# A layernorm's mean and gain applied by VectorE and ScalarE instead of by one matmul a slice

## The reference

```
q, v, g = xn @ Wq, xn @ Wv, xn @ Wg
s[t]  = sigmoid(beta) * s[t-1] + v[t]            # along the sequence, one beta per head
y     = q * s
y     = (y - mean(y)) * rsqrt(var(y) + 1e-5) * ln_g + ln_b     # over the 1024 features
out1  = (y * silu(g)) @ Wo
out2  = mixture of experts of xn: 64 experts, the 8 best per token, two 1024 x 384 up matrices,
        one 384 x 1024 down matrix, silu(h1) * h2; at most 128 token slots per expert
out   = x + out1 + out2
```

## Time and profile before

| what | value |
|---|---|
| median of 3 runs | 2562.5 us |
| the profiled execution | 2563.26 us |
| its span, first to last instruction | 2561.6 us |
| TensorE matmul busy | 2499.2 us, 98% |
| VectorE busy | 1641.4 us, 64% |
| ScalarE busy | 1320.4 us, 52% |
| GpSimd busy | 679.1 us, 27% |
| mean DMA rate | 236 GB/s |
| TensorE's granted clock | 0.991 of full speed |

### The profile page before, as it was taken

How to read it: one execution, slowest core, us unless ns; L and a number is a source line. 1 busy time by engine, 2 the same in 40 slices (tenths; PEclk the granted TensorE clock), 3 DMA queues, 4 the chain that set the end, 5 groups by cost and what they waited for, 6 DMA issues and landing times.

```text
span 2561.6 us, 39307 instructions
## 1 busy us (share of the span) xinstructions
PE 2499.2 (98%) x13625; PEld 2214.0 (86%) x13625; DVE 1641.4 (64%) x1725; ACT 1320.4 (52%) x1499; POOL 679.1 (27%) x523
## 2 busy tenths in 40 slices
PE   7999999899999999999999999999999999999997
PEld 6888977898889988899888898888988889988897
DVE  6776798665566656666665666656665566656654
ACT  4556422464446644556444555545654456544554
POOL 2221122123222222321333222322233232323311
PEclk9999999999999999999999999999999999999998
DMA  7785754696667967669766698666985668866686
GB/s 264 253 296 186 238 202 151 219 312 215 218 219 242 293 235 226 214 221 315 245 230 203 201 317 266 208 212 206 295 286 192 224 220 277 271 227 226 196 269 166
DMA packets 151791, 605.75 MB, mean 236 GB/s; under 512 B 20592, under 2 KB 37040, under 8 KB 151216
## 3 DMA queue, kind: packets, MB, share of 16 engines
q1 hardware_dynamic: 116304, 518.91, 56.5%
q0 software_dynamic: 35424, 86.00, 16.3%
HBM read 520.89 MB, written 100.70 MB: 243 GB/s over the span
## 4 chain that ended last, share of the span: by engine, by line
PE 87%; DVE 7%; ACT 2%; DMA 2%; issue 1%; POOL 0%; SPq 0%; DVEq 0%; ACTq 0%; POOLq 0%
PE psA L1509 17%; PE psA L1511 17%; PE psA L1510 17%; PE psH L1509 7%; PE psH L1511 6%; PE psH L1510 6%; PE psY L1509 4%; PE psY L1511 4%; PE psY L1510 3%; PE psX L1616 2%; PE psY L1541 2%; DVE top L1112 1%; PE psX L1636 1%; DVE keys L1118 1%; DVE pw_lo L1123 1%
## 5 line engine op out<-in xcount | busy, mean ns | idle before, releaser
L1128 DVE TENSOR_TENSOR ew_lo<-ew_raw,ew_hi 128x1536 fp32r<-128x1536 f32 x384 | 693.5, 1816 | 340.8 <-ACT ew_hi L742 326.7
L742 ACT ACTIVATE ew_hi<-ew_raw 128x1536 fp32r<-128x1536 f32 x384 | 568.2, 1483 | 156.4 <-DMA ew_raw<-ew_dram 118.6
L1509 PE MATMUL psA<-xT_hi,pw_hi 128*128 128x512 f32 x1536 | 621.2, 404 | 9.3 <-DVE xT_lo L1043 4.8
L736 ACT ACTIVATE pw_hi<-pw_raw 128x1024 fp32r<-128x1024 f32 x254 | 266.2, 1060 | 672.9 <-PE psA L1511 671.8
L1511 PE MATMUL psA<-xT_hi,pw_lo 128*128 128x512 f32 x1536 | 610.3, 397 | 0.0
L1510 PE MATMUL psA<-xT_lo,pw_hi 128*128 128x512 f32 x1536 | 606.3, 395 | 0.0
L1123 DVE TENSOR_TENSOR pw_lo<-pw_raw,pw_hi 128x1024 fp32r<-128x1024 f32 x256 | 313.4, 1234 | 176.4 <-ACT pw_hi L736 170.4
L1509 PE MATMUL psH<-ew_hi,gT_hi 128*128 128x384 f32 x1024 | 353.3, 345 | 7.9 <-DVE ew_lo L1128 7.1
L1509 PEld LDWEIGHTS psA<-xT_hi,pw_hi 128*128 128x128 f32 x1536 | 290.6, 189 | 72.2 <-DVE xT_lo L1043 5.0
L1511 PEld LDWEIGHTS psA<-xT_hi,pw_lo 128*128 128x128 f32 x1536 | 291.4, 190 | 70.4
L1510 PEld LDWEIGHTS psA<-xT_lo,pw_hi 128*128 128x128 f32 x1536 | 294.0, 191 | 64.0
(11 more groups left out here) (163 smaller groups left out, 3358.4 us busy)
## 6 DMA issues: line engine op xcount, KB each, us to landing
ew_raw<-ew_dram SPq DMA_DIRECT2D x384, 768.0 KB, 6.3
pw_raw<-proj_w_dram SPq DMA_DIRECT2D x256, 512.0 KB, 5.2
xn_scratch<-xt SPq DMA_DIRECT2D x33, 512.0 KB, 4.8
xt<-x_dram SPq DMA_DIRECT2D x32, 512.0 KB, 6.0
out_dram<-x_dram SPq DMA_DIRECT2D x32, 512.0 KB, 6.2
out_dram<-ot POOLq DMA_DIRECT2D x32, 512.0 KB, 12.5
xn<-xn_turned SPq DMA_DIRECT2D x29, 512.0 KB, 4.0
xn_turned<-xraw SPq DMA_DIRECT2D x28, 512.0 KB, 5.1
```

Source lines behind the costliest of these rows:

```text
L736: act.activation(dst[:, slot, :, :], pw_raw[:, slot, :, :], ACT.Copy).then_inc(s_pwhi, 1)
L742: act.activation(ew_hi[:, c % 3, :], ew_raw[:, c % 3, :], ACT.Copy).then_inc(s_ewhi, 1)
L1128: dve.tensor_tensor(ew_lo[:, c % 3, :], ew_raw[:, c % 3, :], ew_hi[:, c % 3, :].bitcast(F32), ALU.subtract).then_inc(s_ewlo, 1)
L1509: pe.matmul(dst, l_hi, r_hi_, start=first, stop=False)
```

## The change

In place of ln6T there is `sel`, two stationary tiles of ones, made once (GpSimd sets four columns, TensorE transposes two tiles, ScalarE copies them). Two matmuls a block (`spread`) multiply them by tok6T, so that bank 0 of psY holds each token's mean on all 128 partitions and bank 1 its deviation. Per slice VectorE then subtracts bank 0 from yb (`center`), ScalarE writes bank 1 times ln_b into `bs`, a buffer of two tiles in SBUF (`std_of`), and `shift_in` computes yb * ln_g + bs. A subtraction is issued one slice ahead of the shift that uses it. The waits on s_sh and s_t move from `shift` on TensorE to `std_of` on ScalarE; the wait of output_mm on the eighth shift stays. The cut diff; the hunks of blocks 0 and 1 place the calls as the text says there: std_of right after gate from slice 3 on in block 0 (0 and 1 after the router step of slice 2), and after gate in block 1.

```diff
+            pool.wait_ge(s_clear, 1)
+            for i in range(2):
+                for r in (0, 2):
+                    o = pool.memset(sel0[:, i, 3 * i + r:3 * i + r + 1], 1.0)
+            o.then_inc(s_clear, 1)
...
+            def std_of(j, m):
+                if isinstance(m, int) and m == 0:
+                    act.wait_ge(s_sh, j + 1)
+                if m >= 2:
+                    act.wait_ge(s_t, KC * j + m - 1)
+                ps = psH if isinstance(j, int) and j == 0 else psY
+                act.activation(bs[:, m % 2, :], ps[:, 1, :], ACT.Copy, scale=ln_b[:, m:m + 1]).then_inc(s_bs, 1)
...
                 gate(j, 2)
+                std_of(j, 0)
+                std_of(j, 1)
                 z_hi_of(j, 0)
                 z_hi_of(j, 1)
                 G(5)
                 gate(j, 3)
+                std_of(j, 2)
+                std_of(j, 3)
                 z_hi_of(j, 2)
                 hidden_part(e + 1)
                 G(6)
                 gate(j, 4)
+                std_of(j, 4)
+                std_of(j, 5)
                 hT_hi_of(e + 1)
                 z_hi_of(j, 3)
                 piece_hi(e + 2, 0)
                 G(7)
                 gate(j, 5)
+                std_of(j, 6)
+                std_of(j, 7)
                 z_hi_of(j, 4)
...
+            def center(j, m):
+                ps = psH if isinstance(j, int) and j == 0 else psY
+                dve.tensor_tensor(yb[:, m, :], yb[:, m, :], ps[:, 0, :], ALU.subtract).then_inc(s_u, 1)
+
             def shift_in(j, m):
-                dve.wait_ge(s_sh, KC * j + m + 1)
-                ps = psH if isinstance(j, int) and j == 0 else psY
-                dve.scalar_tensor_tensor(yb[:, m, :], yb[:, m, :], ln_g[:, m:m + 1], ps[:, m % 2, :],
+                if m == 0:
+                    dve.wait_ge(s_sh, j + 1)
+                    center(j, 0)
+                if m + 1 < KC:
+                    center(j, m + 1)
+                dve.wait_ge(s_u, KC * j + m + 1)
+                dve.wait_ge(s_bs, KC * j + m + 1)
+                dve.scalar_tensor_tensor(yb[:, m, :], yb[:, m, :], ln_g[:, m:m + 1], bs[:, m % 2, :],
                                          ALU.mult, ALU.add).then_inc(s_t, 1)
...
-            def shift(j, m):
-                if m > 1:
-                    pe.wait_ge(s_t, KC * j + m - 1)
+            def spread(j):
+                pe.wait_ge(s_t6, j + 1)
                 ps = psH if isinstance(j, int) and j == 0 else psY
-                pe.matmul(ps[:, m % 2, :], ln6T[:, m, :], tok6T[:, :], start=True, stop=True
-                          ).then_inc(s_sh, 1)
+                for i in range(2):
+                    o = pe.matmul(ps[:, i, :], sel[:, i, :], tok6T[:, :], start=True, stop=True)
+                o.then_inc(s_sh, 1)
...
-                pe.wait_ge(s_t6, j + 1)
                 pe.wait_ge(s_ys, e + 1)
-                shift(j, 0)
-                shift(j, 1)
+                spread(j)
                 g_proj(j, 3)
-                shift(j, 2)
-                shift(j, 3)
                 hidden_mm(e + 1)
                 g_proj(j, 4)
                 hidden_turn(e + 1)
-                shift(j, 4)
-                shift(j, 5)
                 g_proj(j, 5)
-                shift(j, 6)
-                shift(j, 7)
                 g_proj(j, 6)
                 pe.wait_ge(s_t, KC * (j + 1))
```

More of the change, by code:

```diff
@@ L123, in build @@
         tok6T = place("tok6T", [P, TB], F32R)
-        ln6T = place("ln6T", [P, KC, P], F32R)
+        sel = place("sel", [P, 2, P], F32R)
+        bs = place("bs", [P, 2, TB], F32)
         xn = place("xn", [P, KC, P], F32)
@@ L168, in build @@
         top8 = place("top8", [P, 8], F32)
-        ln2 = place("ln2", [P, 2, KC], F32)
-        ln2_hi = place("ln2_hi", [P, 2, KC], F32R)
-        ln6 = place("ln6", [P, KC, P], F32)
+        sel0 = place("sel0", [P, 2, P], F32)
         l1 = place("l1", [P, SLOTS], F32)
@@ L240, in build @@
         s_t6 = sem("s_t6")
-        s_ln = sem("s_ln")
         s_lnT = sem("s_lnT")
@@ L244, in build @@
         s_sh = sem("s_sh")
+        s_u, s_bs = sem("s_u"), sem("s_bs")
         s_t = sem("s_t")
@@ L552, in _ @@
             pool.memset(mk[:, :, :], 0.0)
-            pool.memset(ln6[:, :, :], 0.0).then_inc(s_clear, 1)
+            pool.memset(sel0[:, :, :], 0.0).then_inc(s_clear, 1)
+            pool.wait_ge(s_clear, 1)
[3 more added lines that the diff above has]
+            o.then_inc(s_clear, 1)
             inv_std(3)
@@ L831, in _ @@
                     act.wait_ge(s_lnT, 1)
-                    act.activation(ln6T[:, :, :], chunks(psX), ACT.Copy).then_inc(s_l6, 1)
+                    act.activation(sel[:, :, :].rearrange("p i c -> p (i c)"), psX[:, 0, 0:2 * P], ACT.Copy).then_inc(s_l6, 1)
             square(0, KC // 2 - 1, 1)
@@ L836, in _ @@
                 gate(0, m)
+                if m >= 3:
+                    std_of(0, m - 1)
+                if m == KC - 1:
+                    std_of(0, m)
                 router_step(NTILE - KC + m)
@@ L840, in _ @@
                 if m == 2:
+                    std_of(0, 0)
+                    std_of(0, 1)
                     z_hi_of(0, 0)
@@ L882, in _ @@
                     rows6(1)
+                if m == 2:
+                    std_of(1, 0)
+                if m >= 2:
+                    std_of(1, m - 1)
+                if m == KC - 1:
+                    std_of(1, m)
                 if m == 2:
@@ L1222, in xT_lo_of @@
                                   ALU.subtract).then_inc(s_xlo, 1)
[L1224 to L1237, removed]
             stats_tile(0)
@@ L1282, in _ @@
                 if p == 0:
-                    gain_rows()
                     shift_of(3)
@@ L1684, in _ @@
                 if p == 1:
-                    pe.wait_ge(s_ln, 3)
+                    pe.wait_ge(s_clear, 2)
                     pe.wait_ge(s_plo, NT + 1)
-                    for k in range(KC):
-                        o = pe.transpose(psX[:, k // 4, (k % 4) * P:(k % 4 + 1) * P], ln6[:, k, :], ident[:, :])
+                    for i in range(2):
+                        o = pe.transpose(psX[:, 0, i * P:(i + 1) * P], sel0[:, i, :], ident[:, :])
                     o.then_inc(s_lnT, 1)
@@ L1694, in _ @@
                     token_sums(0)
-                elif m > 2:
-                    shift(0, m - 1)
                 router_step(NTILE - KC + m)
@@ L1700, in _ @@
                 elif m == 2:
[L1701 to L1704, removed]
+                    spread(0)
             for mm in range(KC // 2):
@@ L1726, in _ @@
                 elif m == 2:
[L1727 to L1732, removed]
+                    spread(1)
             pe.wait_ge(s_lf, 1 + SLOTS // 8)
```

## The result

| | before | after |
|---|---|---|
| median of 4 runs | 2563.6 us (2560.4 to 2565.0) | 2609.9 us (2607.7 to 2611.5) |
| ratio, 95% interval | | 1.0187 [1.0174, 1.0199] |
| span of the profiled execution | 2561.6 us | 2605.9 us |
| pitch of the steady blocks (mean of five) | 327.84 us | 334.25 us |

Slower, as forecast, but by 46.3 us where I had said 29.9, and outside my range.

What follows compares the result with a forecast made beforehand. TensorE, busy for 98% of the span, was taken as the bound. Six steady blocks 24.0, block 1 4.9, block 0 and set-up 1 sum to 29.9 us; on 2562.5 that gives 2592 us, range 2574 to 2603.

Steps and rivals of the forecast that it cites:

- First wait: Gate stage of blocks 2 to 7, before the expert's weight piece 3: TensorE would go on 2.7 us later.
- Second wait: Blocks 2 to 7: output product waits until shifts leave psY; 2.3 us wait, both delays together +4.0 us a block.
- Do shifts take turns with GpSimd?: Blocks 2 to 7: scalar_tensor_tensor was to wait for GpSimd, 0.74 up to 1.8 us; sign: some take 1.3 us or more.
- Sum of the two waits: Gate stage of blocks 2 to 7: +4.0 us a block, 24.0 us in six blocks.
- Blocks 0 and 1: Block 1: eight VectorE subtractions on the path to the gather, +4.9 us; block 0 and set-up: std copies and others, +1.
- The pitch of 332: Distance between token transposes of consecutive steady blocks (2 to 7) was to grow from 328 to 332 us.
- Only the second wait grows: Blocks 2 to 7: piece 3 as late as now, output product 1.3 us later a block; 2576 us, chance 0.12.
- matmuls only: Blocks 2 to 7: waits covered, 48 matmul slots saved, 11.0 us faster, 2551.5 us; chance 0.05.
- z_lo(4) wins: Blocks 2 to 7: GpSimd's z_lo(4) gets ahead of gate product 5, a further 1 us a block; 2598 us, chance 0.1.
- The shifts don't take turns: Blocks 2 to 7: shifts are not held by GpSimd, 18.6 us in six blocks; 2587 us, chance 0.2.

Runs made afterwards that it cites:

- experiment 2: Changed kernel with GpSimd's z_lo of slices 0 to 2 held back until VectorE has split piece 3, blocks 2 to 7: 2599.6 us, 1.0144.
- experiment 7: Piece 3 first: expert's piece 3 split ahead of shifts 2 and 3, blocks 2 to 7; changed kernel 2565.5 us (1.0014), kernel before 2553.2 us (0.9969).
- 8: Changed kernel with three moves (weight split before z_hi, shifts 6 and 7 early, piece 3 first): 2556.4 us; silu and hidden product also ahead of piece 5: 2547.8 us.
- Experiment 1: The fill: changed kernel with 14 unused matmuls between the expert's pieces 2 and 3 in blocks 2 to 7: 2594.3 us, 1.0134.
- 4: Changed kernel with ScalarE's weight split, gate 3 and std copies 2 and 3 ahead of z_hi(0) and (1), blocks 2 to 7: 2601.5 us, 1.0164.
- experiment 3: Kernel before plus eight unused VectorE subtractions a block: 1.0189; kernel before plus eight unused ScalarE copies a block: 0.9994.

## Why the prediction was wrong

By its own steps, the predicted 29.9 us against the spans' 44.3:

- **First wait.** Predicted: TensorE goes on 2.7 us later. Measured: 3.05 - 0.47 = 2.58. The chain was the one described: ScalarE's split at 756.70 stands behind z_hi and no longer behind TensorE, GpSimd's z_lo at 756.28 holds VectorE's split for 0.9 us. Removing the turns (experiment 2) gave back 1.1 us.

```profile
755.56 1.24 ACT L804 ACTIVATE z_hi<-yb 128x512 fp32r<-128x512 f32 x2 [3.37 <-DVE yb L1220]
756.70 1.04 ACT L740 ACTIVATE pw_hi<-pw_raw 128x1024 fp32r<-128x1024 f32 x1
```

- **Second wait.** Predicted 2.3 us, net of slots +1.3; measured 2.01 and +1.08. Right, a little too large.
- **Do shifts take turns with GpSimd?** Yes, but they lose less than I gave them. The pair of shifts 6 and 7 takes 1.85 us in block 2 where two undisturbed ones take some 1.4 (0.67 from start to start, 0.75 the last), and the longest of all 64 is 1184 ns, not 1.3 us or more; before, with one operand in PSUM, the maximum was 747:

```profile
L1213 DVE SCALAR_TENSOR_TENSOR yb<-yb,ln_g,bs x64: 739/748/1184, 220.0 to 2459.5; 128x512 f32<-128x512 f32 x64
```

Shift 6 starts at 787.99, while GpSimd has a z_lo from 787.13 to 788.62. The rule of the Trainium skill that was weighed (SBUF — State Buffer, Who interferes with whom) agrees with this trace for this form too; it was worth some 0.43 us at the bank.
- **Sum of the two waits.** (2.58 + 1.08) x 6 = 22.0 us, predicted as 24.0.
- **Blocks 0 and 1.** Up to block 2 the kernel after is 6.3 us later (743.25 against 736.98), predicted 5.9. Inside, the split is another: block 0 ends 1.7 us later (predicted 1) and the gather another 2.7 (predicted 4.9), to be read against the earlier trace rows; 1.8 us come behind the gather, where nothing was predicted and the first wait for piece 3, before block 2, grew from 0.6 to 2.0 us. The stretch scatters by as much between executions, so this agrees and proves little.

```profile
270.43 0.58 PE L1535 MATMUL psA<-pw_hi,z_hi 128*128 128x256 f32 x1 [2.39 <-DVE z_lo L1251]
...
486.04 1.06 PE L1642 MATMUL psX<-ident,xg 128*128 128x128 f32 x8 [2.46 <-DMA xg<-xn_scratch,g_idx]
```

- **The step that failed** is the sum of the steady blocks, where a wait is entered as what it lasts: "TensorE goes on at 759.95, not at 757.22: +2.7 us", and everything behind it at the old pace. Six blocks took 38.0 us more (five pitches some 32, the last block to the end of the span 6), of which waits and slots are 22.0. The other 16.0 us are TensorE's pace at the granted clock of 0.50, a term that the sum did not have; 22.0 + 16.0 + 6.3 are the spans' 44.3. The 16.0 are what is left over, not measured by themselves, and hold to some 4 us, as the sum of waits and slots is up to 0.6 us a block off elsewhere (experiments 7 and 8). Experiment 1 takes most of it away with the waits in place, experiment 2 shows two pitches of the same work, and in experiment 7 the plain sum of waits and slots is enough once the clock is full. The pitch of 332 that was named as the sign of the forecast is what the kernel has with the fill (331.94).

The Trainium skill describes the gate (TensorE: Matmul & The Clock Gate, Part 1: The HAM clock gate): half the pulses are passed after idleness, and the hardware watches on a schedule that doesn't start with the kernel. The trace agrees with the level of 0.50, and the alternating pitches of experiment 2 would fit a schedule that runs on its own; no run here shows the schedule itself. The steady blocks of before gave no sign of it, their waits are at most 1.1 us. But the trace of before did have rows for it, and one of them stands behind a wait that the prediction itself read, the 3.18 us before 465.63:

```profile
466.20 0.41 PE L1511 MATMUL psA<-pw_hi,z_lo 128*128 128x256 f32 x1
466.41 0.41 PE L1509 MATMUL psA<-pw_hi,z_hi 128*128 128x256 f32 x1
...
468.93 0.29 PE L1510 MATMUL psA<-pw_lo,z_hi 128*128 128x256 f32 x1
469.05 0.29 PE L1511 MATMUL psA<-pw_hi,z_lo 128*128 128x256 f32 x1
```

```profile
466.00:468.00 2.00, 2.00 (x11) 2.00 (x11) 2.00 (x4) 0.56 (x1) 0.00 (x0) 0.50 0.74 242
469.00:471.00 2.00, 2.00 (x18) 2.00 (x18) 1.78 (x6) 0.63 (x1) 0.44 (x1) 1.00 0.00 0
```

Matmuls of one form start 0.21 us apart up to 468.54 and 0.12 us apart from 468.69 on; the granted clock is 0.50 in the first stretch and 1.00 in the second. Twelve such distances at the slower pace are 1.1 us lost. In the last expert, behind a wait of 3.76 us, the form 128x512 starts 0.43 us apart where it needs 0.23:

```profile
2542.88 0.55 PE L1636 MATMUL psX<-ident,hh 128*128 128x128 f32 x3 [3.76 <-DVE hh L1133]
...
2546.05 0.63 PE L1509 MATMUL psY<-ew_hi,hT_hi 128*128 128x512 f32 x1
2546.47 0.63 PE L1510 MATMUL psY<-ew_lo,hT_hi 128*128 128x512 f32 x1
```

From 2545.20 to 2550.73 that is 2.5 us lost in thirteen distances. An estimate from these two rows would have put 1.1 to 2.5 us a block behind the predicted wait of 4 us, 7 to 15 us in six blocks, and the forecast of 2592 at 2599 to 2607 us; 2609.9 was measured. Behind the 2.71 us before 481.61 the clock was down too (0.55 in 482.00:484.00), so the second predicted wait, of 2.3 us, could have had a term of its own. The stated range was also not its own sum: 2598 with the upper ends of blocks 0 and 1 (1.1 and 2 us more) is 2601.5, not 2603, and the result lies above both.

**Rivals.** "Only the second wait grows" and "matmuls only" are out by the first wait's 26.9 us; "z_lo(4) wins" is out too, for gate product 5 took its 0.69 us. "The shifts don't take turns" is out by the 1184 ns, though in size the truth lay between it and the forecast. No case held the term that decided.

## What to carry to other kernels

Where TensorE never pauses, a new wait is to be priced twice: its length, and the matmuls behind it, which may run at half pace; here waits of two microseconds and more cost some 3 us a block on top, in blocks with two of them. Look for the longest waits anywhere in the trace, also outside the stage at hand, and read the distances of the matmuls behind them. When TensorE's busy time grows while its instructions get fewer, read the granted clock before anything else. And where a tight engine receives new work, first move what TensorE waits for (here one piece of weights) ahead of it in the queue: that one move was worth 7.1 us a block in the changed kernel and 1.4 in the old.

## What the runs showed of the hardware that was not expected

- The granted clock behind a wait, in the steady blocks: at 0.50 behind every wait of 2.86 us or more in all the kernels here, behind some of those of 2.0 us (of blocks 2 to 6, three of five after and in experiments 2 and 4, one of five in experiment 1) and behind four of five of 2.3 us (experiment 3); at 1.00 behind all of 0.9, 1.1 and 1.6 us. A stretch costs 1.2 to 1.8 us, a long one 1.8 to 2.7 (2.35 by the matmuls in block 2 of the kernel after). The clock can fall when TensorE is already at work again: in block 3 of experiment 2 it starts at 1097.32 behind its wait of 3.05 us, and the clock is 1.00 in 1097.40:1098.30 and 0.50 in 1098.40:1099.40. Why a wait of 2.0 us has such a stretch behind it in one block and not in the next is open.
- A scalar_tensor_tensor with both tensors in SBUF is held by a GpSimd instruction as a tensor_tensor is: 1184 ns at most for a median of 748, against 735 to 747 throughout with one tensor in PSUM.
- Kernels whose code before block 2 is the same reach it at different times: the kernel after at 743.25, with piece 3 first at 746.82, with the fill at 743.14, with all three moves and the early hidden product at 735.57, though these edits begin only in block 2. The pitches within one execution agree to some 0.1 us wherever the clock is full. Why the first stretch scatters is open; the clock has some part in it, for in 66.00:75.00 it is at 0.50 with piece 3 first and at 1.00 in the kernel after.
